# First attention of a four-stage decoder: gate features stacked into 96 rows, and new orders on four engines

## The reference

```python
x = layernorm(x)
q = x @ Wq.T + bq;  k = ctx @ Wk.T + bk;  v = ctx @ Wv.T + bv     # 16 heads of 64
pos = log of differences and ratios of boxes                     # [128 x 128 x 4]
emb = concat([sin(100 * pos * f), cos(100 * pos * f)])           # 16 features a pair, f in (1, 1/31.6)
g = relu(emb @ Wg.T + bg)                                        # a gate per head and pair
mn = softmax(log(clip(g, 1e-6)) + q @ k.T / 8)
x = x0 + tanh(g_xattn[0]) * ((mn @ v) @ Wo.T + bo)
```

## Time and profile before

| what | us |
|---|---|
| median of three runs | 1198.27 (1196.78 to 1199.34) |
| profiled execution, its own time | 1199.1 |
| its span, from the first to the last instruction | 1197.2 |
| PE busy (matmul) | 966.9, 81% |
| DVE busy | 824.2, 69% |
| POOL busy | 722.1, 60% |
| ACT busy | 683.6, 57% |

### The profile page before, as it was taken

One profiled execution on the slowest core, in us unless ns is written; L12 is line 12 of the kernel. 1 busy time (PEld: TensorE's weight loads), 2 busy tenths in 40 slices (PEclk: granted clock), 3 DMA queues, 4 the chain that ended last, 5 costly groups with the idle time before them and its releaser, 6 DMA issues.

```text
span 1197.2 us, 32870 instructions
## 1 busy us (share of the span) xinstructions
PE 966.9 (81%) x12178; PEld 780.5 (65%) x12178; DVE 824.2 (69%) x1947; ACT 683.6 (57%) x1338; POOL 722.1 (60%) x811
## 2 busy tenths in 40 slices
PE   0459899999999974688967399964999999899995
PEld 0346766667777753535634288844888888888885
DVE  3997887788778747568767889945555555555553
ACT  2457888888888862165346388844444444444442
POOL 2988888867766741045413589846555665566563
PEclk9879999999999986689989599966999999999998
DMA  9286766787677763500011000105451135731141
GB/s 280 59 203 125 143 147 149 146 182 145 156 163 129 146 165 55 186 1 1 1 41 32 1 2 21 38 19 195 122 140 31 28 96 139 237 66 26 30 133 19
DMA packets 52117, 119.65 MB, mean 100 GB/s; under 512 B 7616, under 2 KB 30144, under 8 KB 51632
## 3 DMA queue, kind: packets, MB, share of 16 engines
q0 software_dynamic: 14144, 35.48, 20.4%
q1 hardware_dynamic: 35520, 80.71, 20.1%
q10 hardware_dynamic: 2352, 2.10, 0.5%
HBM read 212.54 MB, written 37.85 MB: 209 GB/s over the span
## 4 chain that ended last, share of the span: by engine, by line
PE 41%; DVE 22%; POOL 11%; issue 10%; ACT 8%; DMA 5%; DVEq 1%; SPq 0%; ACTq 0%; POOLq 0%
PE bank L2105 9%; PE bank L2119 7%; POOL PT L560 5%; PE bank L1784 5%; PE bank L1687 3%; DVE nmx L1177 2%; ACT EX L1393 2%; PE bank L1726 2%; PE bank L1764 2%; DVE h L1063 2%; DVE hf L1291 2%; ACT hm L1628 2%; PE bank L1935 2%; DVE PT L923 1%; PE bank L1719 1%
## 5 line engine op out<-in xcount | busy, mean ns | idle before, releaser
L1621 ACT ACTIVATE yg<-bank,bms 128x128 f32<-128x128 f32 x312 | 104.9, 361 | 127.3 <-PE bank L2105 106.5
L1296 DVE TENSOR_TENSOR hm<-hf,hm 128x256 f16<-128x256 f32 x156 | 69.1, 443 | 152.8 <-ACT hm L1628 152.4
L707 POOL DMA_INDIRECT out_x<-ys,sidx x39 | 62.8, 1610 | 111.6 <-DVE ys L1310 111.6
L2105 PE MATMUL bank<-xT,wm_even 128*128 128x128 f16 x1920 | 117.6, 221 | 14.0 <-DVE hf L1291 12.3
L2105 PEld LDWEIGHTS bank<-xT,wm_even 128*128 128x128 f16 x1920 | 111.0, 99 | 19.8 <-DVE hf L1291 14.5
L2105 PE MATMUL bank<-xT,wm_odd 128*128 128x128 f16 x1824 | 111.5, 221 | 14.1 <-DVE hf L1291 11.9
L2105 PEld LDWEIGHTS bank<-xT,wm_odd 128*128 128x128 f16 x1824 | 105.0, 99 | 19.4 <-DVE hf L1291 14.1
L1628 ACT ACTIVATE hm<-hf 128x256 f16<-128x256 f32 x156 | 64.5, 414 | 86.0 <-DVE hf L1291 86.0
L560 POOL TENSOR_TENSOR PT<-PT 128x512 f16<-128x512 f32 x64 | 72.2, 1151 | 63.6 <-ACT PT L1419 63.6
L1291 DVE SCALAR_TENSOR_TENSOR hf<-bank,bms,yg 128x128 f32<-128x128 f32 x312 | 94.1, 342 | 9.2 <-ACT yg L1621 9.0
L619 POOL TENSOR_TENSOR h<-h 128x512 f16<-128x512 f32 x32 | 40.5, 1279 | 83.6 <-DVE h L1063 82.2
(11 more groups left out here) (308 smaller groups left out, 2647.0 us busy)
## 6 DMA issues: line engine op xcount, KB each, us to landing
wm_even<-expert_weights SPq DMA_DIRECT2D x60, 1024.0 KB
wm_odd<-expert_weights SPq DMA_DIRECT2D x57, 1024.0 KB
expert_weights<-in_wcat POOLq DMA_DIRECT2D x16, 768.0 KB, 7.9
wsp<-expert_weights SPq DMA_DIRECT2D x16, 768.0 KB, 4.3
wsp<-in_wcat POOLq DMA_DIRECT2D x16, 768.0 KB, 10.4
expert_weights<-wsp SPq DMA_DIRECT2D x16, 768.0 KB, 3.3
Lst<-gate_tables SPq DMA_DIRECT2D x48, 68.0 KB, 5.8
gate_tables<-Lw SPq DMA_DIRECT2D x6, 512.0 KB, 3.3
```

Of the source, the lines that this page charges most:

```text
L707: nc.gpsimd.indirect_dma_start(out=a["out"], out_offset=bass.IndirectOffsetOnAxis(ap=sidx[:, t:t + 1], axis=0), in_=ys[:, t % 2, :], in_of ...
L1296: v.tensor_tensor(hm16[:, par, 1, c - 1:c + 1, :], hf[:, q % 2, :, :], hm16[:, par, 0, c - 1:c + 1, :], ALU.subtract).then_inc(m_hl, 1)
L1621: s.activation(yg[:, c % 4, :], bank[c % 4][:, 0:MT], ACT.Gelu, bias=bms[:, par, c:c + 1]).then_inc(m_g, 1)
L2105: ins = t.matmul(bank[c % 4][:, w * MT:(w + 1) * MT], wm16[par][:, wp, col:col + P], xT16[:, par, xp * KD + kk, :], start=(n == 0), stop=( ...
```

## The change

The host arranges the boxes, the constants and the gate weights so that the 128 feature rows come as 4 groups of 32 rows, each for 4 of the 16 tokens. SP copies the high part of each group twice and the low part once into `Fst`, 96 rows a group (`stack_high`, 8 transfers of 32 rows x 2 KB, and `stack_low`, 4). The weights `We16` get 96 rows: high, low, high. One product of 96 rows and 64 columns (16 heads x 4 tokens) then adds all three pairs for 4 tokens. `F16s` loses its second parity.

The negation of the half experts moves from ACT to DVE, one operation of 3072 columns. `bo` is scaled by the tanh once, POOL adds it to `X` (`out_bias`), and `residual` becomes one operation. The lists of PE, DVE and ACT get new orders, and `pv` waits for each quarter of the low parts by itself. The loads of `boxm` become two of 1 MB instead of four that broadcast rows; `We` is loaded with 96 x 64 values.

```diff
+QN = 4
+QR = 2 * QN * 4
+FR = 3 * QR
+STK = 16 * 3 * (NN // QN)
...
-        F16s = sb("F16s", [P, 2, 2, NJ * N], F16, l0)
+        F16s = sb("F16s", [P, 2, NJ * N], F16, l0)
+        Fst = sb("Fst", [P, NN // QN, NJ * N], F16, l0)
...
+            def stack_high(b):
+                sp.wait_ge(s_fhi, b + 1)
+                if b:
+                    sp.wait_ge(s_gf, 4 * b)
+                for q in range(NN // QN):
+                    for k in range(2):
+                        sp.dma_start(Fst[k * QR:k * QR + QR, q, :], F16s[q * QR:q * QR + QR, 0, :]).then_inc(s_fst, 16)
+            def stack_low(b):
+                sp.wait_ge(s_flo, b + 1)
+                for q in range(NN // QN):
+                    sp.dma_start(Fst[2 * QR:3 * QR, q, :], F16s[q * QR:q * QR + QR, 1, :]).then_inc(s_fst, 16)
...
+            stack_high(0)
             store_tables(0)
             for par in range(2):
                 load_tables(par)
+            stack_low(0)
...
+                load_tables(b)
+                stack_high(b - 1)
+                store_half(b // 2 - 1, par)
+                load_half(b // 2, par)
+                stack_low(b - 1)
+            stack_high(B - 1)
             store_half(E - 1, 0)
+            stack_low(B - 1)
...
             def feature_low(n, par):
                 gp.wait_ge(s_fhi, n + 1)
-                nc.gpsimd.tensor_tensor(F16s[:, par, 1, :], fs, F16s[:, par, 0, :], ALU.subtract).then_inc(s_flo, 1)
+                if n:
+                    gp.wait_ge(s_fst, STK * n)
+                nc.gpsimd.tensor_tensor(F16s[:, 1, :], fs, F16s[:, 0, :], ALU.subtract).then_inc(s_flo, 1)
+            def out_bias(c):
+                gp.wait_ge(s_tg, 2)
+                gp.wait_ge(s_xn, c + 1)
+                return nc.gpsimd.tensor_tensor(X[:, c, :], X[:, c, :], bo[:, :], ALU.add)
...
                     half_low(b - 1)
                     probs_low(b - 1)
+                    out_bias(b - 1)
                     feature_low(b, par)
...
             def residual(c):
                 dv.wait_ge(s_op, c + 1)
-                v.tensor_tensor(otmp[:, :], bank[7][:, 0:D], bo[:, :], ALU.add).then_inc(s_opt, 1)
-                dv.wait_ge(s_opt, c + 1)
+                dv.wait_ge(s_flo, min(c + 2, B + 1))
                 xb = X[:, bass.ds(c, 1), :]
-                v.scalar_tensor_tensor(xb, otmp[:, :].unsqueeze(1), tg[:, 0:1], xb, ALU.mult, ALU.add).then_inc(s_xu, 1)
+                v.scalar_tensor_tensor(xb, bank[7][:, 0:D].unsqueeze(1), tg[:, 0:1], xb, ALU.mult, ALU.add).then_inc(s_xu, 1)
+            def half_negated(h):
+                dv.wait_ge(w_ld[h % 2], h // 2 * 16 + 16)
+                v.tensor_scalar(wsp[:, h % 2, :], wsp[:, h % 2, :], -1.0, None, ALU.mult).then_inc(w_ng, 1)
```

ACT and PE:

```diff
                 if c:
                     probs_high(b - 1, c == 1)
+                if has_q:
+                    feature_abs(b + 1, 1 - par)
...
+                    s.activation(warm[:, :], nmx[:, 0:1], ACT.Exp, scale=0.0)
                 if c:
                     take_o(b - 1, c == 1)
                 if has_q:
                     v_high(b + 1, 1 - par, (1,))
+                exps(b, (0, 1), c == 0)
                 if has_x:
                     xn_high(b + 2, par)
-                exps(b, par, c == 0)
+                exps(b, (2, 3), c == 0)
...
-                    for n, (wp, fp) in enumerate(PAIRS):
-                        ins = t.matmul(bk[:, jj * 256:(jj + 1) * 256], F16s[:, par, fp, j * N:(j + 1) * N], We16[:, wp, :], start=False,
-                                       stop=(n == 2), skip_group_check=True)
+                    part = bk[:, jj * 256:(jj + 1) * 256].rearrange("p (h q i) -> p q h i", h=H, q=NN // QN)
+                    for q in range(NN // QN):
+                        ins = t.matmul(part[:, q, :, :], Fst[0:FR, q, j * N:(j + 1) * N], We16[0:FR, :], start=False, stop=True,
+                                       skip_group_check=True)
```

More of the change, by code:

```diff
@@ L874, in row_max, with take_pv @@
                                     AX.X, ALU.max, negate=True).then_inc(s_red, 1)
-            def take_pv(c, first=False):
-                for f in range(4):
+            def take_pv(c, fs_, first=False):
+                for f in fs_:
                     ps = bank[6 + f % 2][:, 0:HS * (DK + 1)].rearrange("p (h d) -> p h d", h=HS)
@@ L896, in take_qk, with take_v @@
                                            ALU.mult, ALU.add).then_inc(s_qe, 1)
-            def take_v(b, first=False):
-                for r in range(2):
+            def take_v(b, rs, first=False):
+                for r in rs:
                     dv.wait_ge(s_qf, 6 * b + 4 + r + 1)
@@ L1021, in _ @@
             ternary_hidden()
-            take_pv(B - 1)
+            take_pv(B - 1, range(4))
             residual(B - 1)
@@ L1812, in iteration @@
                 if c:
[L1813 to L1815 removed]
+                    project_o(b - 1, range(0, CH // 2))
                 scores(b, par, 1)
[L1817 to L1819 removed]
+                if c:
+                    project_o(b - 1, range(CH // 2, CH))
+                for g in range(4):
+                    gate(b, par, g, c == 0, has_q)
             iteration(0, 0, 0, True, True)
```

149 lines of the change are left out of this document (65 added, 84 removed).

## The result

| what | before | after |
|---|---|---|
| median | 1198.69 (1196.78 to 1199.34, 4 runs) | 1243.79 (1241.32 to 1258.48, 4 runs) |
| ratio to before | | 1.0404 [1.0323, 1.0486] |
| profiled execution, own time | 1199.1 | 1243.87 |
| its span | 1197.2 | 1242.0 |
| granted TensorE clock, mean | 0.926 | 0.894 |

The change makes the kernel 45 us slower. I had said 1207.0 and a range of 1173 to 1223: the sign was right, the size was not, and the time lies outside.

What follows compares the result with a forecast made beforehand. Bound moves from PE's order to POOL's list followed by DVE's. Iterations 1 and 2 -1.7, 3 to 6 +5.6, 7 to 13 +0.7, 14 -2.3, 15 and behind +5.7: +8.0 on 1199.1, forecast 1207, range 1173 to 1223.

Steps and rivals of the forecast that it cites:

- The transfers: SP's queue: stack_low lands at 18.5, gate products needed under way at 20.3; no cost while a landing takes under 7.6 us.
- The rival of the late rows: Stacked rows on SP's queue: a landing of 9.5 us is 1.9 late in 14 iterations, +27, 1234 us; chance 0.06.
- Iteration 14: Last iteration but one: no distance to compute, so PE bounds it at 21.3 us, 2.3 won.
- the end: Iteration 15 and behind it: next weights queue behind stack_low(15), negation stands between their sums and probs; +5.7 us.
- Start: First stack_high ahead of the first table stores: 0 of a possible 3.4 us; iterations 1 and 2 together win 1.7.
- The port: DVE's distances beside POOL: one SBUF operation gets in at each change of POOL's operations, 5.7 us instead of 2.1.
- The loop: POOL's list followed by DVE's: 0.7 + 16.0 + 0.3 + 6.6, 23.6 to 23.8 us; 26.5 with tables.
- VectorE's negation: 128x3072 16-bit values on DVE ahead of probs: 0.95 us by bytes, 2.1 by elements; 0.95 taken.
- GpSimd's bias: out_bias, one 128x256 sum added to POOL's list: 0.67 us in the loop, bounds 0.6 to 1.1.
- VectorE's new order: DVE's list behind probs: residual 0.5 us, norm 0.3 and about 1 of waiting, feature_distance reached at about 11.4.
- The short products: PE's gate groups: eight 64-column products make a group 0.68 us instead of 1.08, saving 1.6 us an iteration.
- The first rival: DVE beside POOL: the port does not bind, PE's 21.4 us holds without tables and 23 with; 1174 us, chance 0.30.

Runs made afterwards that it cites:

- e1: Changed kernel with stack_low issued ahead of store_half and load_half on SP's queue instead of behind them; 1221.11 us, 1.0173.
- e8: Kernel before with the 12 transfers of 64 KB an iteration added at the change's places on SP, read by nobody; 1216.57 us, 1.0143.
- e7: e5 with the first table stores ahead of the first stack_high, and the next stage's weight loads ahead of stack_low(15); 1213.04 us, 1.0132.
- e12: Kernel before with value products waiting for each quarter of the low parts and VectorE negating half experts in one operation ahead of probs; 1208.8 us, 1.0078.
- e5: e1 with feature_distance also put back just ahead of the negation; 1216.52 us, 1.0166.
- e9: e7 with ScalarE's copy of the turned rows (xn_high) ahead of exponents 0 and 1 instead of behind them; 1214.79 us, 1.0134.
- e14: Kernel before with the bias alone moved: out_bias on POOL, the residual one VectorE operation at its old place; 1207.83 us, 1.0065.
- e15: Kernel before with VectorE's residual of element b - 1 moved behind probs, still two operations; 1220.95 us, 1.0176.
- e17: e7 with VectorE's residual back at its old place, ahead of the fractions instead of behind probs; 1236.71 us, 1.0305.
- e13: e7 with ScalarE negating the half experts again, in three operations ahead of and between the exponents; 1219.85 us, 1.0164.

## Why the prediction was wrong, by its own steps

**The transfers are the step that failed**: the landing of `stack_low` ahead of the gates, which my sum put at no cost. It cost 22.7 us (e1). I had the gates' rows there at 18.5, 1.8 us before they were needed, by 9.45 + 3.34 + the load's issue + 4 x 0.42 + 5.8 behind the negation. In the iteration shown they are 11.43, 5.30, 4 x 0.6 and 8.44, together 27.5 us from the start of the accumulating transfer, where my sum has 21.1. Two things are mixed in this. The 9.45 was a poor choice: it is the shortest of the 16 accumulating transfers of the kernel before, whose median is 10.42 and longest 12.44. And the terms grew when 12 transfers an iteration joined them: from before to e8, which adds the transfers alone, the medians go from 10.42 to 11.66, for the store from 3.29 to 4.65, and for the load behind it from 4.33 to 6.94 (in the changed kernel 10.94, 4.43 and 5.37). I had taken the median of a landing, although the same sum named 7.6 us as the point from which it costs, and the longest took 9.1. The rival of the late rows was priced at 1234 and given 0.06; it is what happened (e1: 22.7 us, against its 27). It should have had one chance in three: a margin of 1.8 us on a chain of three transfers, all timed without the load that the change adds, is no margin. The waits were not the 1.9 us in each of 14 iterations that the rival had, but up to 7.9 in nine, with PE's slower clock behind them; that its total came so near is partly luck.

**What e1 leaves.** With the rows in time the rest of my sum can be laid beside a trace (us more than in the kernel before, by the ends of `probs`):

| stretch | forecast | e1 | the changed kernel |
|---|---|---|---|
| until `probs(1)`, and iteration 2 | -1.7 | +8.4 | +12.5 |
| 3 to 6, with tables | +5.6 | +7.6 | +11.9 |
| 7 to 13 | +0.7 | +4.7 | +19.6 |
| 14 | -2.3 | -2.3 | +0.5 |
| 15 and behind it | +5.7 | +4.7 | +0.4 |
| all | +8.0 | +23.1 | +44.8 |

So besides the late rows it was the start that I had wrong, by 10 us, and the loop, by 4 in seven iterations without tables. Iteration 14, where DVE has no distances, came out as worked out, and the end within 1 us.

**Start.** The first `stack_high` was taken as 0 of a possible 3.4, as the first gates were said to have that much room; no row showed this. In the changed kernel the last table store, which took 2.6 us from its issue to the loads behind it, took 10.39 behind it (chain of waits):

```profile
68.70 10.39 DMA gate_tables<-R
79.10 0.32 SPq L392
```

From there the chain runs through the table loads, `stack_low(0)`, the load of the first half expert, POOL's list and the accumulating transfer behind it to the gates of element 1, whose low rows land at 125.75. Of the 10.4 us e1 takes away 3.4, which were late rows too, and what e7 adds leaves 5.6, the operations of DVE beside POOL that e7 shows above.

**The port** does what the earlier trace rows showed, and more where tables are made: eight distances take 4.8 to 6.4 us in e1's iterations without tables (5.7 forecast), and 8.6 to 9.1 in those with. The Trainium skill ("SBUF — State Buffer", section "Who interferes with whom") makes the second comer wait until the first's whole instruction is over; I had read it with the earlier trace rows as a turn at each change of POOL's operations. In e12 the floor began only when the low part under way and all four `split_qk` behind it were over, 5.87 us for 0.69 of work, so that reading is too kind, and the wait goes beyond the one instruction of which that section speaks. In the changed kernel the price is smaller (e5 against e1), since there DVE waits for POOL's list in either order: in e7 the fractions are held until 348.63 where in e1 the distances are.

**The loop** of POOL's list followed by DVE's, which I had named, accounts for the iterations without tables: 24.18 in e7 against 23.6 to 23.8. e9 shortened the other wait, for ScalarE, by 0.7 us without gain. POOL's 16.04 had been 16.0. DVE's tail behind it is 7.4 in e7, with the distances in it, where I had 6.6 with the turns; in the changed kernel's own order the distances end at 312.27, 1.4 us behind POOL's list and not 0.3, so that it comes to 24.2 as well. **VectorE's negation** is 0.95 us, as by bytes, but e12 prices it at 9 us. **GpSimd's bias** is 0.72 to 1.19 us (0.67 taken, 1.1 the bound), 8 us in e14. I had added both inside the loop and not at the start, where e12 and e14 lose 4 to 6 us: the first `residual` stands at 116.77 and 118.21 instead of 112.22.

**VectorE's new order**: the residual behind `probs` costs the kernel before 21 us (e15). I had counted its 0.5 us and about 1 us of waiting of `norm` in the list, not what later maxima do to PE. In the changed kernel it is not what costs: there the old place is 24 us worse (e17). **The short products** save 1.7 us by the length of a group (0.66 for 1.08) and 1.9 by PE's busy time in e13, for 1.6 forecast. In a loop of 24.2 us that is idle time of PE; no run has them alone. The first rival (the port does not bind, 1174, chance 0.30) had no support in any run: in e5 and e7, where the distances take 2.13 us again, DVE is held in its fractions instead and iterations take 24.2.

The prices in the kernel before (distances 11, negation 9, bias 8, transfers 17, residual 21) and the late rows (23) add up to 89 us, twice the measured 45, so prices of parts do not add here. e17 shows one such case (the residual's place costs in one order of PE and pays in the other) and the end another (8 of e8's 17 us, but 0.4 in the changed kernel). How the rest offsets each other was not measured.

## What to carry to other kernels

A small transfer that a new wait depends on goes ahead of everything in its queue that itself waits, and its chain is priced with the longest of the rows for each link, not with one of them, and with an allowance for the added load. Two engines that wait for each other at a port can make a loop of one's list and the other's tail; here 0.72 us more on POOL's list cost 0.3 to 0.7 us an iteration and 0.95 on DVE's 0.3 to 0.8, while both showed idle time, and 1.9 us less on PE, the busiest engine, did not keep the iterations of the changed kernel from growing. Moving 0.9 us of work to the head of a list cost 2.3 us an iteration (e15), because what follows it then missed its gap. And the price of a part, measured alone in the old kernel, need not be its price in the new one.

## What the runs showed of the hardware

The issue of a transfer of 32 rows from SBUF to SBUF took 0.59 us on SP (of the table loads 0.42), and its landing 2.0 to 9.1 us. Twelve of them an iteration lengthened the 768 KB transfers beside them by 1.2 to 2.6 us (medians, e8 against before). An operation of DVE that reads and writes SBUF waited through four more operations of POOL behind the one under way (5.87 us in e12). Behind a wait of 3.8 us the granted PE clock went from 1.00 to 0.57 for 8 us (the levels are 2.4 and 1.2 GHz), and 48 products took 4.54 us instead of 2.84.
